# State-space layers of a two-block network on one Trainium2 core: the parameter work of a layer issued one layer further ahead

## The reference, cut to what matters

```python
def _s4d_layer(z, log_dt, A_re_log, A_im, C_re, C_im, D_skip, W, bvec):
    dt = jnp.exp(log_dt)
    A = -jnp.exp(A_re_log) + 1j * A_im          # 32 modes for each of 128 channels
    dtA = A * dt[:, None]
    C = (C_re + 1j * C_im) * (jnp.expm1(dtA) / A)
    K = 2.0 * jnp.einsum('hn,hnl->hl', C, jnp.exp(dtA[:, :, None] * l)).real
    y = irfft(rfft(z, 2 * Lz) * rfft(K, 2 * Lz))[..., :Lz]   # causal convolution
    y = jax.nn.gelu(y + z * D_skip[:, None])
    out = jnp.einsum('oh,bhl->bol', W, y) + bvec[None, :, None]
    return out[:, :Hh] * jax.nn.sigmoid(out[:, Hh:])
for i in range(4):
    z = _layernorm_channels(h, ln_w[i], ln_b[i])
    z = _s4d_layer(z, ...)
    h = h + z
```

## Time and profile before

| | us |
|---|---|
| median of 3 runs | 1274.57 (1274.16 to 1275.48) |
| the profiled execution's own time | 1267.12 |
| its span, first to last instruction | 1265.3 |
| input products of layer 0 start | 70.22 |
| input products of layers 1, 2, 3 start | 155.19, 239.68, 322.36 |
| output products of layers 0, 1, 2, 3 start | 113.82, 198.56, 281.78, 362.60 |

### The profile page before, as it was taken

The page is one execution under the profiler, slowest core; times in us unless marked ns, Lnnn a source line. Parts: engine busy times, 40 slices in busy tenths (PEclk is TensorE's granted clock), DMA queues, the critical chain, the costliest instruction groups (busy, mean ns, idle before and its releaser), DMA issues.

```text
span 1265.3 us, 20116 instructions
## 1 busy us (share of the span) xinstructions
PE 1007.3 (80%) x7980; PEld 682.8 (54%) x7980; DVE 766.9 (61%) x1340; ACT 535.7 (42%) x1240; POOL 418.3 (33%) x488
## 2 busy tenths in 40 slices
PE   6894886858535179999999867769969988979887
PEld 3563654636523067878787753324546643546653
DVE  2575574664827534646463578969946646956654
ACT  4646555366123222221212060006768635668742
POOL 0724403414105600000000043547944444954420
PEclk9766967769667589999999978989989999979999
DMA  3307135063054285253723040000012210011101
GB/s 96 74 7 137 42 53 118 10 102 72 15 88 201 51 158 100 74 125 48 134 47 69 0 161 1 0 0 1 1 34 57 76 67 26 1 34 43 44 18 33
DMA packets 60480, 76.50 MB, mean 60 GB/s; under 512 B 37501, under 2 KB 41993, under 8 KB 58633
## 3 DMA queue, kind: packets, MB, share of 16 engines
q1 hardware_dynamic: 60396, 75.36, 26.1%
HBM read 52.87 MB, written 1.51 MB: 43 GB/s over the span
## 4 chain that ended last, share of the span: by engine, by line
PE 50%; DVE 16%; POOL 14%; ACT 6%; SPq 5%; DMA 4%; issue 4%; POOLq 0%; DVEq 0%
PE psum L1189 7%; PE psum L1191 6%; PE psum L1190 6%; POOL rest L1441 3%; POOL rest L1431 3%; POOL rest L1437 2%; PE psum L693 2%; PE psum L1684 2%; SPq L1012 2%; PE psum L1677 2%; DVE main L506 2%; SPq L1018 2%; ACT rest L1375 2%; PE psum L1730 2%; DMA rest<-share_d 2%
## 5 line engine op out<-in xcount | busy, mean ns | idle before, releaser
L406 POOL TENSOR_TENSOR kept<-kept 128x8 f32<-128x8 f32 x8 | 1.6, 204 | 400.4 <-DVE kept L383 400.4
L1375 ACT ACTIVATE rest<-psum,main 128x128 f32<-128x128 f32 x256 | 113.4, 480 | 11.5 <-POOL main L1452 8.9
L1036 ACT ACTIVATE x_high<-main 128x512 fp32r<-128x512 f32 x48 | 30.4, 634 | 199.0 <-DVE main L1110 199.0
L1189 PE MATMUL psum<-x_high,w_low 128*128 128x512 f32 x192 | 76.8, 400 | 19.9 <-DVE x_low L1115 19.9
L1467 POOL TENSOR_TENSOR rest<-rest,main 128x512 f32<-128x512 f32 x64 | 65.4, 1044 | 44.1 <-DVE main L1537 44.1
L1189 PE MATMUL psum<-hid_high,w_low 128*128 128x512 f32 x192 | 75.6, 394 | 0.7 <-DVE main L1134 0.7
L1190 PE MATMUL psum<-x_low,w_high 128*128 128x512 f32 x192 | 76.1, 397 | 0.0
L1191 PE MATMUL psum<-x_high,w_high 128*128 128x512 f32 x192 | 76.1, 397 | 0.0
L1190 PE MATMUL psum<-hid_low,w_high 128*128 128x512 f32 x192 | 74.8, 389 | 0.0
L1191 PE MATMUL psum<-hid_high,w_high 128*128 128x512 f32 x192 | 74.7, 389 | 0.0
L1110 DVE TENSOR_TENSOR main<-kept,rest 128x512 f32<-128x512 f32 x48 | 33.1, 690 | 67.8 <-PE psum L1191 43.8
(11 more groups left out here) (319 smaller groups left out, 2807.2 us busy)
## 6 DMA issues: line engine op xcount, KB each, us to landing
rest<-share_d SPq DMA_DIRECT2D x4, 3072.0 KB, 21.3
rest<-share_d SPq DMA_DIRECT2D x4, 2304.0 KB, 20.2
main<-main SPq DMA_DIRECT2D x32, 256.0 KB, 5.2
main<-k_pad SPq DMA_DIRECT2D x16, 512.0 KB, 7.4
rest<-main SPq DMA_DIRECT2D x32, 256.0 KB, 3.5
main<-w_dram SPq DMA_DIRECT2D x2, 3072.0 KB, 14.0
main<-rest SPq DMA_DIRECT2D x32, 128.0 KB, 4.4
rest<-tables_dram SPq DMA_DIRECT2D x2, 2048.0 KB, 9.1
```

The source lines that it names most:

```text
L1189: T.matmul(dst, w_small, x_large, start=first, stop=False)
L1375: last = A.activation(probs[:, p, 4 * r + m, :], bank[2 * p + r][:, m * P:(m + 1) * P], ACT.Exp, scale=row_scale[:, c, r, m:m + 1], bias=r ...
```

## The change

All parameter work is issued a layer earlier. K, the Toeplitz matrices, all 16 back groups of layer 0 and the powers of layer 1 are made before layer 0 starts; so are the near angles of layer 2. In layer L, between its input and its output products, the kernel matmuls and backs of layer L + 1 run, and the exponents, magnitudes and powers of layer L + 2. The rates and residues of all four layers are computed at once at the start, from one DMA. The magnitudes now lie in banks 4 to 7, so the output products of layers 0 and 1 wait for DVE's powers of layer L + 2. EARLY becomes (16, 16, 10, 10): of layer 1's backs all stand ahead of layer 0's output products, of those of layers 2 and 3 ten do and six follow. Near turns (L + 3) and far turns (L + 2) on DVE follow the yT transpose; the copies of `turns` as scratch for the phases move to `s_b` and `b_re`. SP issues u first, then k rows of L + 1, and after the output products the Toeplitz matrices and the powers. The core of the diff, with a line "..." where lines are left out:

```diff
+        NEAR_FIRST, FAR_FIRST = (4, 4, 4, 0), (0, 6, 6, 6)
+        PRODUCTS = ("near0", "far0", "exp0", "near1", "exp1", "near2", "far1", "exp2", "near3", "far2", "exp3", "far3")
+        PRODUCT = {name: n + 1 for n, name in enumerate(PRODUCTS)}
+        ANGLE = {name: n + 1 for n, name in enumerate(p for p in PRODUCTS if p[0:3] != "exp")}
...
             if more:
-                s4_dve_powers(dve, L + 1, near(LOW_BANKS))
-
-            dve.wait_ge(sem("s4_y"), L * PIECES + PIECES)
+                dve.wait_ge(sem("s4_k_out"), (L + 2) * 64)
             V.transpose(yT.rearrange("p (c i) -> p i c", i=CHUNK), y_act).then_inc(sem("s4_yT"), 1)
+            if L + 3 < S4_LAYERS:
+                s4_dve_near_turns(dve, L + 3)
+            if L + 2 < S4_LAYERS:
+                s4_dve_far_turns(dve, L + 2)
 
...
         def s4_pe_layer(pe, L, more):
+            if L == 0:
+                pe.wait_ge(sem("s4_turns"), ANGLE["near2"])
+                s4_pe_far_angles(pe, 1)
+            if L and L + 2 < S4_LAYERS:
+                s4_pe_exponents(pe, L + 2)
             if more:
-                s4_pe_near_angles(pe, L + 1, (2, 3))
...
+                pe.wait_ge(sem("s4_in"), L + 1)
+                pe.wait_ge(sem("s4_pow"), (L + 2) * 3)
+                s4_pe_kernel(pe, L + 1)
+                s4_pe_back(pe, L + 1, range(EARLY[L + 1]))
+            if L == 0:
+                pe.wait_ge(sem("s4_turns"), ANGLE["far1"])
+                s4_pe_exponents(pe, 2)
+
+            if L + 2 < S4_LAYERS:
+                pe.wait_ge(sem("s4_pow"), (L + 3) * 3)
             pe.wait_ge(sem("s4_toep_in"), L * 16 * PIECES + 16 * PIECES)
...
             if more:
-                pe.wait_ge(sem("s4_pow"), (L + 2) * 3)
-                if L + 2 < S4_LAYERS:
-                    s4_pe_dta(pe, L + 2, RATES)
-                s4_pe_back(pe, L + 1, range(EARLY))
+                pe.wait_ge(sem("s4_k_rows"), L + 2)
+                pe.wait_ge(sem("s4_back"), (L + 1) * BACKS + EARLY[L + 1])
+            if L + 3 < S4_LAYERS:
+                s4_pe_near_angles(pe, L + 3)
+            pe.wait_ge(sem("s4_y"), L * PIECES + PIECES)
+            if L + 2 < S4_LAYERS:
+                s4_pe_far_angles(pe, L + 2)
+            if more:
+                s4_pe_back(pe, L + 1, range(EARLY[L + 1], BACKS))
 
             pe.wait_ge(sem("s4_yT"), L + 1)
             pe.wait_ge(sem("s4_glu_in"), L * 32 + 32)
-            for b in range(BLOCKS):
+            for b in range(3):
                 s4_pe_glu(pe, L, b)
-                if more:
-                    s4_pe_back(pe, L + 1, range(EARLY + b, EARLY + b + 1))
             if more:
-                if L + 2 < S4_LAYERS:
...
         def s4_act_layer(act, L, more):
             A = nc.scalar
...
+            ahead = L + 2 < S4_LAYERS
+            if ahead:
+                s4_act_sines_near(act, L + 2)
+            if L == 0:
+                s4_act_round_far(act, 1)
+            if L and ahead:
+                s4_act_magnitudes(act, L + 2)
...
-                s4_act_round_far(act, L + 1)
-            if more:
-                s4_act_sines_near(act, L + 1)
                 s4_act_sines_far(act, L + 1)
-                s4_act_magnitudes(act, L + 1, LOW_BANKS)
+                s4_act_back(act, L + 1, range(EARLY[L + 1]))
+                s4_act_k_rows(act, L + 1)
...
+            if L + 3 < S4_LAYERS:
+                s4_act_round_near(act, L + 3)
+            if ahead:
+                s4_act_round_far(act, L + 2)
+            if more:
+                s4_act_back(act, L + 1, range(EARLY[L + 1], BACKS))
             A.activation(warm[:, 3 * L + 3:3 * L + 4], warm[:, 0:1], ACT.Sigmoid)
...
             act.wait_ge(sem("s4_yT"), L + 1)
             act.wait_ge(sem("s4_glu_in"), L * 32 + 32)
-            for b in range(BLOCKS):
+            for b in range(3):
                 s4_act_sigmoid(act, L, b)
-                if more:
-                    s4_act_back(act, L + 1, range(EARLY + b, EARLY + b + 1))
             if more:
-                s4_act_norm(act, L + 1, EARLY + BLOCKS)
+                N = L + 1
+                s4_act_square(act, N, 0)
+                s4_act_sigmoid(act, L, 3)
+                s4_act_square(act, N, 1)
+                s4_act_square(act, N, 2)
+                s4_act_z(act, N, 0)
+                s4_act_square(act, N, 3)
...
+        def s4_pool_layer(pool, chain, L, more):
+
+            s4_pool_decay(pool, L)
+            if more:
+                s4_pool_phases(pool, chain, L + 1)
+                if L + 2 < S4_LAYERS:
+                    s4_pool_coefficients(pool, chain, L + 2)
+                s4_pool_weighted(pool, L + 1)
+                s4_pool_norm(pool, L + 1)
...
+        def s4_sp_layer(sp, L):
+
+            one, more = L + 1, L + 1 < S4_LAYERS
+            for dst, name in ((w_out, "w_out"), (b_out, "b_out")):
+                sp.dma_start(dst, dram[name][L]).then_inc(sem("s4_glu_in"), 16)
+            if more:
+                sp.wait_ge(sem("s4_z_rows"), one * 6)
+                sp.dma_start(ln_wb, dram["ln_wb"][L + 1]).then_inc(sem("s4_ln_in"), 16)
             for ri, src in ((0, u_re), (1, u_im)):
                 sp.wait_ge(sem("s4_u"), L * 2 + ri + 1)
                 for g in range(GROUPS):
                     at = CHUNK + MODES * ri
                     sp.dma_start(zu[at:at + MODES, HG * g:HG * (g + 1), :], src[32 * g:32 * g + 32]).then_inc(sem("s4_u_moved"), 16)
+            if more:
+                s4_sp_k_out(sp, L + 1)
+                sp.wait_ge(sem("s4_tp_free"), one)
+                s4_sp_toeplitz(sp, L + 1)
+                s4_sp_powers(sp, L + 1)
+                sp.wait_ge(sem("s4_h"), one * BLOCKS)
...
             s4_act_round_near(act, 0)
             s4_act_sines_near(act, 0)
             s4_act_round_far(act, 0)
             s4_act_sines_far(act, 0)
-            s4_act_magnitudes(act, 0, HIGH_BANKS)
+            s4_act_magnitudes(act, 0)
             act.wait_ge(sem("cond"), 4)
             ln_act(act, LN_A, z_tok, hT, one_plus[:, 1:2], mod[:, 0:1], first=0)
-            s4_act_dtaT(act, 1, 6)
-            s4_act_back(act, 0, range(EARLY))
-            s4_act_norm(act, 0, EARLY)
+            s4_act_round_near(act, 1)
+            s4_act_back(act, 0, range(BACKS))
+            s4_act_sines_near(act, 1)
+            s4_act_k_rows(act, 0)
+            s4_act_square(act, 0, 0)
+            s4_act_square(act, 0, 1)
+            s4_act_magnitudes(act, 1)
+            s4_act_square(act, 0, 2)
...
             pe.wait_ge(sem("x_in"), 16)
             pe.wait_ge(sem("cond"), 4)
-            pe.sem_inc(sem("s4_tp_free"), 1)
+            pe.wait_ge(sem("s4_turns"), ANGLE["far0"])
...
+            pe.wait_ge(sem("s4_pow"), 3)
+            s4_pe_near_angles(pe, 1)
-            pe.wait_ge(sem("s4_pow"), 3)
-            s4_pe_dta(pe, 1, 6)
-            s4_pe_back(pe, 0, range(EARLY))
-            pe.wait_ge(sem("s4_dtaT"), 2)
-            s4_pe_norm(pe, 0, EARLY)
+            s4_pe_back(pe, 0, range(BACKS))
+            s4_pe_kernel(pe, 0)
+            pe.wait_ge(sem("s4_turns"), ANGLE["near1"])
+            s4_pe_exponents(pe, 1)
+            pe.wait_ge(sem("s4_k_rows"), 1)
+            pe.wait_ge(sem("s4_back"), BACKS)
+            s4_pe_first_norm(pe)
+            pe.wait_ge(sem("s4_pow"), 6)
+            s4_pe_near_angles(pe, 2)
...
```

More of the change, by code:

```diff
@@ L243, in program @@
         decay = keep(HG, CHUNKS)
-        tanh = [keep(HG) for _ in range(2)]
-        r_chunk = [keep(HG) for _ in range(2)]
         small = [keep(HG) for _ in range(14)]
@@ new lines, in s4_dve_near_turns, with s4_dve_far_turns @@
+        def s4_dve_near_turns(dve, G):
+            dve.wait_ge(sem("s4_rounded"), ANGLE[f"near{G}"])
+            first = NEAR_FIRST[G]
+            nc.vector.scalar_tensor_tensor(turns, turns, MAGIC, near(psum[:, 512 * first:512 * first + NEAR_COLS]),
+                                           ALU.subtract, ALU.subtract).then_inc(sem("s4_turns"), 1)
+        def s4_dve_far_turns(dve, G):
+            dve.wait_ge(sem("s4_rounded"), ANGLE[f"far{G}"])
+            nc.vector.scalar_tensor_tensor(far_turns, far_turns, MAGIC, far_of(FAR_FIRST[G]), ALU.subtract, ALU.subtract).then_inc(sem("s4_turns"), 1)
@@ L585, in s4_dve_layer, with s4_pe_dta @@
                     V.scalar_tensor_tensor(xT[:, sl], hT[:, sl], gate[:, 2:3], xT[:, sl], ALU.mult, ALU.add).then_inc(sem("x_s4"), 1)
-        def s4_pe_dta(pe, G, where):
-            pe.wait_ge(sem("s4_dta"), G * 2 + 1)
-            nc.tensor.transpose(bank[where][0:2 * HG, 0:P], dta[G % 2].rearrange("p a h -> p (a h)"), ident).then_inc(sem("s4_dtaT_ps"), 1)
-        def s4_pe_near_angles(pe, G, ks):
-            for k in ks:
-                last = nc.tensor.matmul(bank[4 + k][:, :], dtaT[HG:2 * HG], expo[HG:2 * HG, 512 * k:512 * k + 512], start=True, stop=True)
-                if k == 3:
-                    last.then_inc(sem("s4_x_ps"), 1)
+        def s4_pe_dta(pe, where):
+            pe.wait_ge(sem("s4_dta"), 1)
```

(13 more changed lines are left out.)

424 lines of the change are left out of this document (205 added, 219 removed).

## The result

| | before | after |
|---|---|---|
| median, 13 runs each | 1273.3 (1268.0 to 1278.8) | 1267.08 (1260.73 to 1269.37) |
| ratio to before | | 0.9942 [0.9924, 0.9959] |
| profiled execution, span | 1267.12, 1265.3 | 1262.45, 1260.7 |
| input products of layers 0 to 3 start | 70.22, 155.19, 239.68, 322.36 | 111.25, 193.36, 261.00, 326.22 |
| output products start | 113.82, 198.56, 281.78, 362.60 | 153.16, 224.82, 291.76, 356.94 |

The account below looks back on a forecast made before the run. Output products were taken to wait for u's DMA behind Toeplitz issues, the next input products for PE, then DVE's norm and copies. Prologue +43.3 less savings in fronts and tails gave +10.1: 1274.57 to 1284.7 us, own range 1279 to 1291, widened 1273 to 1294.

Parts of the forecast that it names:

- prologue: Before layer 0's input products: parameter work reappears there with nothing beside it, input products at 113.5 instead of 70.2, +43.3 us.
- fronts of layers 0 to 3: Input to output products: -1.2 us in layer 0; layers 1 to 3 fall to 32.6, giving -10.8, -9.5, -7.6.
- tails of layers 0 to 2: Output products to next input products, fewer backs but a later first sigmoid: 0, -0.7, then -1.0 and -2.4 us.
- copies 6.31: DVE's two copies at the end of each norm, taken to last 6.31 us as in the earlier trace.
- the rest are rows within 1 us: Prologue: bound given to every step of the chain except the three angle and exponent products (3.8 or 7.2 by clock).
- from the first sigmoid to the input products: Tails: PE's stream laid out without the twelve backs takes 24.8 us, against 28.7 before.
- u's landing: Layers 1 to 3: u's last transfer starts at 29.1, lands between 31.2 and 33.4, taken as 32.6 after the input products.
- Layer 0: Its output products wait for DVE's powers (2) and start 42.4 us after the input products, before 43.6: -1.2.
- The clock: Prologue's 32-row PE products: 7.2 us each for near angles (1) and (2) after idling, 4.5 for exponents (1).
- The rival that had these products fast: 32-row products run at 2.4 GHz because PE is busier: -10.2 us, time 1274.5, no change; chance 0.11.
- Norm shrinks more: Tails of layers 0 to 2: each removed back group saves 0.9 us, not 0.4; -12 more, 1272.7; chance 0.15.
- ACT or PE ends last: Fronts of layers 1 and 2: at 1.2 GHz ACT or PE outlasts the 2 us cover; +12, 1296; chance 0.13.

Follow-up runs that it names:

- Experiment 6: Changed kernel plus eleven unread 128x512 matmuls on PE ahead of near angles (2) in the prologue; 1259.54 us, ratio 0.9899 to the kernel before.
- Experiment 4: Changed kernel with all 16 back groups ahead of the output products in layers 1 and 2 too; 1268.76 us, ratio 0.9964 to the kernel before.
- experiment 1: Changed kernel plus two unused 128x1024 GpSimd operations beside DVE's copies in the norms of layers 1 to 3; 1275.61 us, ratio 1.0002 to the kernel before.
- Experiment 2: Kernel before, with the last two GpSimd phase products moved ahead of the norm in layers 1 to 3; 1258.59 us, ratio 0.9904.
- Experiment 3: Changed kernel with the Toeplitz DMAs of layers 1 to 3 issued ahead of u's again; 1299.98 us, ratio 1.0224 to the kernel before.
- experiment 12: Kernel before, with GpSimd's phase products moved away from DVE's copies in all four norms; 1254.16 us, ratio 0.9845.

## Why the prediction was wrong

The sum was made of nine terms; the -1.0 and -2.4 of layer 2's tail are one entry here. Each against the trace, in us relative to before:

| step | forecast | measured |
|---|---|---|
| prologue | +43.3 | +41.0 |
| fronts of layers 0 to 3 | -1.2, -10.8, -9.5, -7.6 | -1.7, -11.9, -11.3, -9.5 |
| tails of layers 0 to 2 | 0, -0.7, -3.4 | -1.2, -4.9, -6.1 |
| sum | +10.1 | -5.6 |

**The step that failed is "copies 6.31" from the earlier trace rows.** I took an instruction's duration as its own. It was 1.8 us of copying and 4.5 of waiting for GpSimd, and the change moved GpSimd's neighbour away. The step stands in the prologue's norm, under "the rest are rows within 1 us", and in all three tails, through the 24.8 us "from the first sigmoid to the input products". With 3.43 in place of 6.31 that stretch is 21.9; measured are 22.3 (first sigmoid at 171.11) and 21.8 (at 239.20), so the rest of that layout was right. In the sum this is 2.9 us four times, 11.5 of the 15.7 that it was off: with it right the sum is -1.4, so the sign turns on this step. The other 4.2 us are the fronts, 5.3 us shorter than forecast, and smaller terms of both signs. Against it stand 1.7 in the prologue, for the small copy that waited too (1.86 instead of 0.19), and 1.2 in the tail of layer 0, where the first sigmoid came 10.1 us after the last gelu, not 8.9. That tail was 40.2 us long in this execution and 36.2 and 36.3 in the profiles of experiments 6 and 4, where the same code ran at a higher clock, so its entry is a draw as well. Experiments 1 and 2 show the step from both sides. That the phases on GpSimd move too follows from "All parameter work is issued a layer earlier", and it was not priced at all: the move of an engine's work was asked only for what it waits for and issues, not for what it ran beside.

**u's landing, 3.5 taken, 2.36 measured, and its last transfer begun 28.3 us behind the input products (289.27 less 261.00), not 29.1.** Together they make the 1.8 us in layers 2 and 3 (32.6 forecast, 30.8 and 30.7 measured). Landing and issue time (5.84 us for eight, not 7.01) both came from rows of a loaded queue, and the chosen value between 2.1 and 4.3 should have been nearer the lower end, since the change empties the queue ahead of it. In layer 1 this didn't end last: DVE's powers did, at 31.5 after the input products (31.2 was the figure given for them). Experiment 3 confirms what hangs on the queue: 30 us.

**Layer 0** waited as forecast: its output products idled 8.43 us for DVE's powers (2) and started 41.9 us behind the input products. The forecast's own terms there add up to 41.6 and not to 42.4, and in the tail of layer 0 24.8 and 8.9 against 34.1 are -0.4, which was entered as 0. Neither matters for the miss.

**The clock** was right for near angles (1) and (2), 7.19 each, and 0.8 too dear for exponents (1). Experiment 6 agrees with the reason given, idling ahead. That the first norm's length hangs on the clock too, by up to 7 us, was not priced. The rival that had these products fast did not come; near (3) got part of it (5.01).

**The prologue** came out 2.3 us shorter than worked out, which is the copies again and the exponents, less the small copy. That it came so near is partly luck: in five profiles with the same prologue code the input products of layer 0 started at 108.5 to 119.0, by the clock and by the copies that the execution drew.

**Rivals.** "Norm shrinks more" forecast 1272.7 and the sign, but by another way: from the removed backs. It needed the stretch from the first sigmoid to the input products to be some 6, 3 and 3 us shorter than my layout; with the copies put right the layout has 21.9 and the traces 22.3 and 21.8, so nothing is left for it. Experiment 4 doesn't test it, since the six groups that it moves stand ahead of the gated linear unit and not in the norm. "ACT or PE ends last" did not occur: in layer 1 DVE's powers ended last, and PE idled 2.24 us for them. The range had 1273.0 as its lower end; the time lies 5.9 below it. Most of the miss is one row that had been given a bound of 1 us.

## What to carry over

A duration in a timeline may contain a wait that no releaser shows. If the same instruction has different durations in different places (a small copy here: 0.19 and 1.86 us), look what GpSimd does beside it, and when work moves on GpSimd, price what it will run beside, not only what it waits for. Before a schedule is rebuilt, try the cheap order first: moving three pairs of GpSimd instructions brought 12 us where the look-ahead of a whole layer brought 7 (intervals overlapping slightly), and clearing all four norms brought 20 (clear of both kernels). A long DMA issue ahead of a short, urgent one costs its full issue time and a longer landing (10 us a layer here). A gain in a stretch whose clock differs from execution to execution is read behind that stretch, not from the start of the trace.

## What the runs showed of the hardware

- VectorE's fp32 copies from SBUF to SBUF (64x512) take 0.9 us each with no large GpSimd instruction beside them, and two take 3.43 beside one 128x992 product, 6.31 beside two of 128x1024, and 3.44 or 10.87 us beside the same row of six. In the last case one copy stood through four products (experiment 1). Small VectorE operations with two SBUF inputs (128x32) went from 0.19 to 1.84 us as well beside GpSimd's phase products (experiment 12's layer 0). In the other direction GpSimd's L910 (128x32, 0.25 us elsewhere) took 1.26 us there beside VectorE's L546 of 1.23 us, which has two SBUF inputs. DVE in experiment 12's layer 0:

```profile
68.74 1.84 DVE L447 SCALAR_TENSOR_TENSOR rest<-rest 128x32 f32<-128x32 f32 x1 [3.90 <-ACT rest L751]
...
75.22 2.44 DVE L539 STREAM_TRANSPOSE rest<-psum 128x512 f32<-128x512 f32 x4
```

  The four transposes out of PSUM in the second row, also beside a phase product (GpSimd's sixth ran from 74.83 for 2.34 us), took 0.61 us each: not slowed (0.72 in the earlier trace rows). The Trainium skill, "SBUF — State Buffer", section "Who interferes with whom", states this rule: VectorE, in a mode that takes both port pairs or with two SBUF inputs, and GpSimd share a pair of ports that one of them holds for a whole instruction, while the other stands. The traces agree, with the numbers above. They show besides that the one that stands may stand through several instructions of the other, as the copy of 8.65 us did.
- The granted clock can be wrong early in a trace. In the changed kernel it reads 1.00 in the first 56 us, while exponents (0) and near angles (1) there took the time they elsewhere have at 0.50:

```profile
27.30:34.40 7.10, 7.10 (x10) 2.47 (x9) 2.10 (x8) 5.75 (x6) 0.00 (x0) 1.00 0.00 0
...
76.70:80.30 3.60, 3.60 (x11) 1.38 (x9) 0.00 (x0) 2.51 (x5) 0.00 (x0) 1.00 0.01 2
80.40:84.00 3.60, 3.60 (x7) 1.49 (x7) 0.00 (x0) 0.61 (x2) 0.00 (x0) 0.53 0.14 29
104.20:111.20 7.00, 7.00 (x8) 2.42 (x8) 0.00 (x0) 0.00 (x0) 6.36 (x15) 0.50 0.00 1
```

  The Trainium skill, "TensorE: Matmul & The Clock Gate", section "Seeing it yourself", warns that the clock's trace events have been unreliable; durations decide here. In the third row the clock falls right behind exponents (1), after 3.7 us of 32-row products at full speed.
- What follows the start of layer 3's output products is the same code in all kernels; it took 902.7 to 909.4 us in the profiled executions, with no cause shown for the spread. A difference of a few microseconds between two single profiles must be read from the stage it is claimed for.
